# Polar factor of a 128x128 matrix: 32 Newton steps inside attention against 17 quintic steps in two later stages

## The reference, cut to what matters

```
x = x + attention(layernorm(x))        # 16 heads of 8, causal, 2 sequences
x = x + experts(layernorm(x))          # 16 experts, capacity N/16, top 1
x = x + scan_block(layernorm(x))
x = x + experts(layernorm(x))

# scan_block
U, _, Vt = svd(W_scan_raw);  W = U @ Vt          # 128 x 128: the polar factor
q = x @ W_up.T;  v = x @ W_v.T
q = scan over time with combine(left, right, W)  # v' = (left + right) @ W, attention over 4 lanes, rms norm
y = (q * v) @ W_proj.T
```

## Time and profile before

| | us |
|---|---|
| median of 3 runs | 1975.16 |
| lowest and highest of them | 1974.81, 1977.96 |
| the profiled execution: its own time | 1976.67 |
| the profiled execution: its span, first to last instruction | 1975.0 |
| mean granted clock of TensorE | 0.921 |

### The profile page before, as it was taken

The page is one execution under the profiler, slowest core; times in us unless marked ns, Lnnn a source line. Parts: engine busy times, 40 slices in busy tenths (PEclk is TensorE's granted clock), DMA queues, the critical chain, the costliest instruction groups (busy, mean ns, idle before and its releaser), DMA issues. The chain is left out here.

```text
span 1975.0 us, 42847 instructions
## 1 busy us (share of the span) xinstructions
PE 1624.5 (82%) x14150; PEld 1057.9 (54%) x14150; DVE 1423.3 (72%) x2559; ACT 952.3 (48%) x2093; POOL 688.7 (35%) x498
## 2 busy tenths in 40 slices
PE   4599989998998998999646648999999999976183
PEld 3233333333333333333435548888889888875173
DVE  6789988888988888987331246888888888874222
ACT  4177777777777776777421122333333333332020
POOL 5400000000000000000144326877777777853632
PEclk9699999999999999999857878999999999996597
DMA  3200000000000000000162151222222222204423
GB/s 115 83 18 19 18 15 16 18 19 20 19 19 12 18 19 20 19 18 2 70 217 73 44 147 35 86 76 79 79 85 78 80 76 85 85 22 147 153 68 104
DMA packets 171647, 117.12 MB, mean 59 GB/s; under 512 B 10940, under 2 KB 161852, under 8 KB 171208
## 3 DMA queue, kind: packets, MB, share of 16 engines
q1 hardware_dynamic: 167368, 106.33, 18.2%
q0 software_dynamic: 4096, 8.46, 1.2%
HBM read 63.98 MB, written 50.72 MB: 58 GB/s over the span
## 5 line engine op out<-in xcount | busy, mean ns | idle before, releaser
L562 DVE TENSOR_REDUCE chunk_max<-ps_max 128x1 f32<-128x512 f32 (+3 forms) x1280 | 703.8, 603 | 103.1 <-PE ps_max L667 56.6
L611 ACT ACTIVATE probs<-ps_s 128x512 f32<-128x512 f32 (+3 forms) x1280 | 612.6, 536 | 215.0 <-PE ps_s L659 106.5
L640 PE MATMUL ps_s<-Qs,Ks 50*128 50x512 bf16 (+3 forms) x1280 | 368.0, 353 | 37.9 <-DVE chunk_max L562 22.0
L650 PE MATMUL ps_max<-Ks,Qs 48*128 48x512 bf16 (+3 forms) x1280 | 377.3, 360 | 13.2 <-POOL a_ident L504 10.6
L712 PE MATMUL ps_o<-probs,Vp 128*32 128x512 f32 (+3 forms) x2560 | 343.9, 562 | 5.2 <-ACT O_sb L594 4.8
L1424 POOL TENSOR_TENSOR lane_products<-L,q 128x1024 f32<-128x1024 f32 x132 | 309.4, 2374 | 3.9 <-DMA L<-scanned 3.9
L519 POOL TENSOR_TENSOR A_b<-A_newton,b_tile 128x128 f32<-128x128 f32 x32 | 14.6, 457 | 811.3 <-ACT A_newton L614 811.3
L640 PEld LDWEIGHTS ps_s<-Qs,Ks 50*128 50x128 bf16 x1280 | 98.4, 93 | 370.0 <-DVE chunk_max L562 313.6
L1479 DVE TENSOR_TENSOR weighted<-exp_scores,psV_s 128x4096 f32<-128x4096 f32 x44 | 194.2, 4413 | 0.2 <-issue 0.2
L1437 POOL TENSOR_TENSOR q<-L,z_normed 128x1024 f32<-128x1024 f32 x44 | 141.5, 3216 | 144.5 <-DVE z_normed L1459 144.5
L1558 PE MATMUL psS<-ident,lane_products 128*128 128x128 f32 x1408 | 169.2, 279 | 23.9 <-POOL lane_products L1424 23.9
(11 more groups left out here) (224 smaller groups left out, 2317.8 us busy)
## 6 DMA issues: line engine op xcount, KB each, us to landing
scanned<-q SPq DMA_DIRECT2D x44, 512.0 KB
L<-scanned SPq DMA_DIRECT2D x44, 512.0 KB
m_w<-in_L_ffn_w_dram SPq DMA_DIRECT2D x32, 512.0 KB
Qs<-q_parts SPq DMA_DIRECT2D x192, 32.0 KB
Ks<-k_parts SPq DMA_DIRECT2D x192, 32.0 KB
dispatched<-m_blank SPq DMA_DIRECT2D x2, 2080.0 KB
m_blank<-dispatched SPq DMA_DIRECT2D x16, 260.0 KB
routed<-m_blank SPq DMA_DIRECT2D x2, 2048.0 KB
```

Source lines behind the costliest of these rows:

```text
L562: nc.vector.tensor_reduce(out, scores[:, 0:w], axis=AX.X, op=ALU.max).then_inc(max_reduced, 1)
L611: nc.scalar.activation(dst, ps_s[(k + r) % R][:, q0:], ACT.Exp, scale=SCALE).then_inc(exp_done, 1)
L640: last = nc.tensor.matmul(ps_s[(k + r) % R][:, q0:], K[r][rows, kt * P:(kt + 1) * P], Q[r][rows, g * QW + q0:(g + 1) * QW], start=True, st ...
L650: last = nc.tensor.matmul(ps_max[(k + r) % R][:, 0:w], Q[r][rows, i * P:(i + 1) * P], K[r][rows, ck * QW:ck * QW + w], start=True, stop=no ...
```

## The change

The Newton steps and everything that belongs to them leave `attend`. A class `Polar` computes 17 quintic steps of the same form with other coefficients, 14 with (3.4445, -4.7750, 2.0315) and then 3 with (15/8, -10/8, 3/8). In one step the copy of A, Z, Y and the copy of S are on VectorE, the copy of the transpose on ScalarE, the four matmuls on TensorE; GpSimd only makes two scaled identities. `moe` m0 runs 12 steps: on VectorE behind `route(1)`, on ScalarE behind `copy_totals(1)`, on TensorE behind `count(1)` and before the first `turn`. `scan_inputs` runs 5: on TensorE behind the turned weights; on VectorE two in front of the first moments and one in front of each of the other three groups of eight tiles; on ScalarE in front of the root. The second expert layer gets an empty list of steps.

```diff
-NEWTON = (15 / 8, -10 / 8, 3 / 8)
+SPREAD = (3.4445, -4.7750, 2.0315)
+SETTLE = (15 / 8, -10 / 8, 3 / 8)
+POLAR = [SPREAD] * 14 + [SETTLE] * 3
+POLAR_FIRST = 12
...
# attend, gpsimd
-            nc.gpsimd.memset(b_tile[:], NEWTON[1])
-            nc.gpsimd.tensor_scalar(a_ident[:], c.ident[:], NEWTON[0], None, ALU.mult).then_inc(made, 1)
...
-                    nc.gpsimd.tensor_tensor(A_b[:], A[:], b_tile[:], ALU.mult).then_inc(newton_pool, 1)
-                    pool.wait_ge(newton_pool, s * 2 + 1)
-                    nc.gpsimd.tensor_tensor(Z[:], A_b[:], a_ident[:], ALU.add).then_inc(newton_pool, 1)
# attend, vector
-                    if k == NEWTON_AA + 1 and exp:
-                        newton(s)
# attend, scalar
-                            nc.scalar.activation(A[:], newton_ps[:, 0:D], ACT.Copy).then_inc(misc_read, 1)
...
-                            nc.scalar.activation(c.S[:].rearrange("p a d -> p (a d)"), newton_ps, ACT.Copy)\
-                              .then_inc(misc_read, 1)
# attend, tensor
-                if k == NEWTON_A:
-                    misc("A")
-                    nc.tensor.matmul(newton_ps[:, 0:D], c.S[:, 0, :], c.S[:, 0, :], start=True, stop=True)\
-                      .then_inc(newton_mm, 1)
-                if k == NEWTON_AA:
-                    misc("Y")
-                    nc.tensor.matmul(newton_ps[:, 0:D], A[:], A[:], start=True, stop=True).then_inc(newton_mm, 1)
-                if k == NEWTON_X:
-                    nc.tensor.matmul(newton_ps[:, 0:D], c.S[:, 1, :], Y[:], start=True, stop=True)
-                    nc.tensor.matmul(newton_ps[:, D:], Y[:], c.S[:, 1, :], start=True, stop=True).then_inc(newton_mm, 1)
...
+class Polar:
+    def on_gpsimd(self, pool):
+        for step, t in self.scaled_ident.items():
+            self.nc.gpsimd.tensor_scalar(t[:], self.c.ident[:], step[0], None, ALU.mult).then_inc(self.made, 1)
+
+    def on_vector(self, dve, i):
+        vector, (_, b, a2) = self.nc.vector, self.steps[i]
+        dve.wait_ge(self.made, 2)
+        dve.wait_ge(self.A_in_psum, i + 1)
+        vector.tensor_copy(self.A[:], self.ps_A).then_inc(self.A_read, 1)
+        vector.scalar_tensor_tensor(out=self.Z[:], in0=self.ps_A, scalar=b, in1=self.scaled_ident[self.steps[i]][:],
+                                    op0=ALU.mult, op1=ALU.add).then_inc(self.A_read, 1)
+        dve.wait_ge(self.AA_in_psum, i + 1)
+        dve.wait_ge(self.A_read, 2 * i + 2)
+        vector.scalar_tensor_tensor(out=self.Y[:], in0=self.ps_AA, scalar=a2, in1=self.Z[:], op0=ALU.mult, op1=ALU.add)\
+              .then_inc(self.Y_done, 1)
+        dve.wait_ge(self.X_in_psum, 2 * i + 1)
+        vector.tensor_copy(self.c.S[:, 0, :], self.ps_X).then_inc(self.S_copied, 1)
+
+    def on_scalar(self, act, i):
+        act.wait_ge(self.X_in_psum, 2 * i + 2)
+        self.nc.scalar.activation(self.c.S[:, 1, :], self.ps_XT, ACT.Copy).then_inc(self.ST_copied, 1)
+
+    def on_tensor(self, pe, i):
+        tensor, S, S_T = self.nc.tensor, self.c.S[:, 0, :], self.c.S[:, 1, :]
+        if i:
+            pe.wait_ge(self.S_copied, i)
+        tensor.matmul(self.ps_A, S, S, start=True, stop=True).then_inc(self.A_in_psum, 1)
+        pe.wait_ge(self.A_read, 2 * i + 1)
+        tensor.matmul(self.ps_AA, self.A[:], self.A[:], start=True, stop=True).then_inc(self.AA_in_psum, 1)
+        pe.wait_ge(self.Y_done, i + 1)
+        if i:
+            pe.wait_ge(self.ST_copied, i)
+        tensor.matmul(self.ps_X, S_T, self.Y[:], start=True, stop=True).then_inc(self.X_in_psum, 1)
+        tensor.matmul(self.ps_XT, self.Y[:], S_T, start=True, stop=True).then_inc(self.X_in_psum, 1)
+
+    def tensor_done(self, pe):
+        pe.wait_ge(self.S_copied, len(self.steps))
+        pe.wait_ge(self.ST_copied, len(self.steps))
...
# moe: banks are the four halves of psH
+            if polar_steps:
+                polar.on_gpsimd(pool)               # before the blank rows are made
...
             route(1)
+            for i in range(len(polar_steps)):
+                polar.on_vector(dve, i)
...
             pe.wait_ge(steps_done, 5 + HALF_STEPS + 7)
+            if polar_steps:
+                pe.wait_ge(xsT_copied, NCH)
+                for i in range(len(polar_steps)):
+                    polar.on_tensor(pe, i)
+                polar.tensor_done(pe)
...
# scan_inputs, vector
+            for i in range(NPOLAR - SC + 1):
+                polar.on_vector(dve, i)
             for ch in range(SC):
+                if ch:
+                    polar.on_vector(dve, NPOLAR - SC + ch)
                 dve.wait_ge(summed, ch + 1)
...
# scan_inputs, tensor
             pe.wait_ge(wT_copied, 2)
+            for i in range(NPOLAR):
+                polar.on_tensor(pe, i)
+            polar.tensor_done(pe)
```

More of the change, by code:

```diff
@@ L440, in reads @@
             if not isinstance(s, int) or s > 0:
-                order = ["rows1", "A", "comb", "Y", "rows0", "X", "end"]
+                order = ["rows1", "comb", "rows0", "end"]
                 if not nxt:
                     order.remove("rows0")
-                return s * 6 + order.index(name)
-            return ["rows0 of head 0", "rows1", "A", "Y", "rows0", "X", "end"].index(name) if s == 0 else 0
+                return s * 3 + order.index(name)
+            return ["rows0 of head 0", "rows1", "rows0", "end"].index(name) if s == 0 else 0
         @block.sync
@@ L547, in normalise @@
                   .then_inc(misc_read, 1)
-            def newton(s):
-                dve.wait_ge(newton_mm, s * 3 + 2)
-                dve.wait_ge(newton_pool, s * 2 + 2)
-                nc.vector.scalar_tensor_tensor(out=Y[:], in0=newton_ps[:, 0:D], scalar=NEWTON[2], in1=Z[:],
-                                               op0=ALU.mult, op1=ALU.add).then_inc(misc_read, 1)
             def section(s, j, r, p, exp, nxt):
@@ L762, in between @@
                 if k == COMBINE_FIRST:
-                    misc("X")
+                    misc("end")
                     combine(s, 0)
-                if k == NEWTON_X:
-                    nc.tensor.matmul(newton_ps[:, 0:D], c.S[:, 1, :], Y[:], start=True, stop=True)
-                    nc.tensor.matmul(newton_ps[:, D:], Y[:], c.S[:, 1, :], start=True, stop=True).then_inc(newton_mm, 1)
             def section(s, j, r, p, exp, nxt):
@@ L830, in _, with __init__ @@
             dve.wait_ge(y_done, NCH)
+class Polar:
+    def __init__(self, nc, c, sb, sem, steps, banks):
+        self.nc, self.c, self.steps = nc, c, steps
+        self.A, self.Y, self.Z = (sb(n, [P, D]) for n in ("A_polar", "Y_polar", "Z_polar"))
+        self.scaled_ident = {step: sb(f"ident_{n}", [P, D]) for step, n in ((SPREAD, "spread"), (SETTLE, "settle"))}
+        self.ps_A, self.ps_AA, self.ps_X, self.ps_XT = (bank[:, 0:D] for bank in banks)
+        (self.made, self.A_in_psum, self.A_read, self.AA_in_psum, self.Y_done, self.X_in_psum, self.S_copied,
+         self.ST_copied) = (sem(n) for n in ("polar_made", "A_in_psum", "A_read", "AA_in_psum", "Y_done", "X_in_psum",
+                                             "S_copied", "ST_copied"))
+    def on_gpsimd(self, pool):
[32 more added lines that the diff above has]
+        pe.wait_ge(self.ST_copied, len(self.steps))
@@ L905, in moe @@
         y_sent = [sem(f"y_sent{u}") for u in range(2)]
+        polar = Polar(nc, c, sb, sem, polar_steps, [psH[0][:, 0:512], psH[0][:, 512:], psH[1][:, 0:512], psH[1][:, 512:]])
         block = cx.enter_context(nc.Block())
@@ L1071, in _ @@
             copy_totals(1)
+            for i in range(len(polar_steps)):
+                polar.on_scalar(act, i)
             def copy_rows(e):
@@ L1232, in scan_inputs @@
             sem(n) for n in ("xn_ready", "xT_in_psum", "xT_copied", "q_in_psum", "v_in_psum", "q_copied", "v_copied"))
+        polar = Polar(nc, c, lambda n, shape: sb(n + "_b", shape), sem, POLAR[POLAR_FIRST:],
+                      [psQ[:, 0:512], psQ[:, 512:], psV[:, 0:512], psV[:, 512:]])
+        NPOLAR = len(POLAR) - POLAR_FIRST
         block = cx.enter_context(nc.Block())
@@ L1255, in _ @@
         def _(pool):
+            polar.on_gpsimd(pool)
             for ch in range(SC):
```

28 lines of the change are left out of this document (6 added, 22 removed).

## The result

The changed kernel takes 1998.95 us (median of 4 runs, 1996.04 to 2000.16) and the kernel before 1976.47 (4 runs beside it, 1974.81 to 1977.96). The ratio is 1.011, interval 1.0098 to 1.0122: 22.5 us slower, where I had forecast 11.7. The profiled execution took 1999.71 us around a span of 1997.7.

A forecast was written before the change was run, and what follows sets the result against it. No engine was busy throughout; VectorE's row maxima set the attention's pace. Attention -11.4, first expert layer +8.0 and scan inputs +15.1 gave +11.7 us, taking the 1975.16 median to 1986.9; range 1981 to 1991, extended down to 1977.

The forecast's parts named there:

- part 1: Attention: removing 32 Newton steps saves 0.34 us a head for 31 heads, plus start and end: -11.4 us, bounds 0 to -25.5.
- A, Y and X: Three Newton places in each attention head, whose removal was to save 0.04, 0.10 and 0.20 us.
- The start: In front of the attention loop, TensorE no longer waits for the scaled identity: 0.4 us saved, bounds 0 and 0.6.
- the last head: Attention's final head, with no maxima to hide Newton work under: 0.5 us saved, bounds 0 and 1.3.
- nothing is added here, so a loss is excluded: Attention: claim that removing the Newton steps could not cost time, so the gain's lower bound was 0.
- The price of a step: One serial polar step: three matmul legs of 0.90 us and three VectorE operations of 0.28, 3.54 us; 2.61 at higher clock.
- part 2: First expert layer: 12 polar steps outlast the 34.0 us hole before the first gathered tile: +8.0 us, bounds 0 and 10.
- Part 3: Scan's input stage: 5 polar steps in VectorE's queue delay the moments: +15.1 us, bounds 11.4 and 16.
- The clock: TensorE's granted clock in both polar chains was taken to stay at 0.50, the 1.2 GHz level; forecast there given 0.79.
- the first rival: Clock rises in both polar chains, hiding the expert-layer steps and cutting the scan's cost to 11.4: 1975 us; chance 0.11.
- The second rival: Attention: Newton matmuls cause the whole of the 0.33 and 0.23 us gaps, saving 25.5 us: 1972.8 us; chance 0.06.
- the third: Scan's moments hide the polar steps, which then cost VectorE 4.2 us instead of 15.1: 1976 us; chance 0.04.

The follow-up runs named there:

- e1: Changed kernel with all 17 polar steps left out, only the Newton removal kept: 0.9989 of the kernel before, -2.2 us.
- e16: Changed kernel with 70 already-met waits on TensorE in the fourth and fifth heads of the attention loop's body: 1.0087 of the kernel before.
- e9: Changed kernel with 64 semaphore increments at the start of TensorE's attention stream: 1.0208 of the kernel before.
- e14: Changed kernel with 64 semaphore increments at the start of TensorE's attention stream, repeated on another chip: 1.0104 of the kernel before.
- e7: Changed kernel with its 17 steps spread over four places (2, 9, 3, 3); intended empty instructions absent from the built program: 0.9998 of the kernel before.
- e15: Changed kernel with its 17 steps spread over four places (2, 9, 3, 3), no padding, on another chip: 0.9988 of the kernel before.
- e10: Changed kernel with 128 semaphore increments at the start of TensorE's attention stream: 1.0296 of the kernel before.
- e11: Kernel before with 96 semaphore increments at the start of TensorE's attention stream: 1.0078 of the unpadded kernel before.
- e12: Changed kernel with steps spread over four places (2, 9, 3, 3) and 64 semaphore increments on TensorE in the attention: 1.0139 of the kernel before.
- e2: Changed kernel keeping the 12 steps of the first expert layer, the 5 beside the scan's moments left out: 1.0033 of the kernel before, +6.5 us.

## Why the prediction was wrong

**The size of part 1 is the step that failed.** I had -11.4 us; alone it measured -2.2 (e1). That lies within the bounds written beside the term, 0 and -25.5, but the range of the forecast kept only -8 to -16 of them. The working behind it was sound for a plain head: A, Y and X were to give 0.04, 0.10 and 0.20, and the traces of all the kernels with the new attention show 0.03 to 0.04, 0.08 and 0.19, at those steps, 0.30 for 0.34. The start (0.1 to 0.9 us earlier over the traces, for 0.4) and the last head (0.5 where no stall falls into it) came near the forecast too. What was wrong is "nothing is added here, so a loss is excluded": I multiplied one head by 31 and never looked at the heads that hold the turn of the loop, though the earlier trace rows give 26.70 as the average and the timeline of a plain head 26.15. The difference, some 17 us in all, was the loop's turn, and that loss grew with the changed stream of instructions by 4.2 us in the traced run and by 6.5 in e1. In the traced run 3.2 of the 4.2 are in the last heads of the passes, where the stall is, and the rest in the heads behind them. That a fetch delays a 4 KB store, and the store TensorE, is shown by e16 and the late pairs of all traces; that the turn is dearer when a fetch comes just ahead of it rests on three built streams with that pattern (e9 and e14, e16, e7 and e15), and is argued. Why TensorE stands idle a second time behind the turn in e10, e11 and e12 stays open, and so does the rest of what e1 lost: its attention ended 2.8 us ahead of the kernel before, and its last instruction 0.2 us behind.

**The price of a step** was 3.54 us and is 3.61: the leg of A takes 0.91 from matmul to VectorE, the other two 0.84, and each hop from VectorE to TensorE 0.34. Twelve of them make part 2 8.7 instead of 8.0, in the trace and in the runs (e2 less e1).

**Part 3** was 15.1 and is 14.9 in the trace, 16.2 in the runs. The order of the steps and the moments is as forecast: 7.1 us in front of the first bn_stats (1149.24 to 1156.38), then 4.1 us from group to group.

**The clock** stayed at 0.50 in both chains from the second matmul on, so the first rival is out. Around the first, the clock had risen for 3.4 us, from 1008.3 to 1011.7, where the kernel before had 0.50 throughout. The forecast tied this rival to what the Trainium skill says of copies, TensorE: Matmul & The Clock Gate (Loop structure matters more than you think): that they don't break the warmth. The changed kernel hardly tests it, since TensorE was idle for 2.8 us between the first A and the next matmul. The three steps behind the last expert do, and the traces differ. They began at 2.4 GHz with steps of 2.68 us (2.61 forecast). In e7 all three ran so, but in e15, the same built program, the second step's last matmuls were at 1.2 GHz again, from 1123.12 on, though no idle time of TensorE between was over 0.7 us. So a chain that once runs fast need not stay fast here.

**The second rival** (the gaps close wholly) is out with 0.30 us a head, and **the third** with the 14.9 us of part 3.

**A term I didn't have** is where the low clock falls in stages that the change doesn't touch. In the changed kernel it met the scan's tail:
```profile
1786.60:1790.00 3.40, 3.40 (x19) 3.40 (x18) 1.85 (x4) 1.06 (x3) 0.84 (x1) 0.50 0.00 0
```
The same stretch of the kernel before, for comparison:
```profile
1786.60:1790.00 3.40, 2.29 (x18) 2.05 (x17) 1.22 (x1) 1.02 (x1) 2.03 (x1) 0.90 0.00 0
```
The scan took 598.2 to 602.5 us over the traces, and the expert loop took from 0.9 us less to 2.2 more than in the kernel before. With the turns this may be why one profile can be 3 us off a median. It is an explanation that fits the rows; no run tested it.

The sum with the measured terms: -2.2 + 8.7 + 16.2 = 22.7, against 22.5. The sign and two of the three terms held. The range did not: the lower bound of part 1, no gain at all, stood in the text and would have given 1975.16 + 8.0 + 15.1 = 1998.3, but the range ended at 1991.

## What to carry to other kernels

Read a loop's gain in the passes, not in its plain part: count the heads that hold the turn separately, and treat their cost as unknown by several us for any change to TensorE's stream there, because its instruction fetches can hold up small transfers that someone waits for. A serial chain costs its full length beyond its cover and nothing within it: 17 steps at 3.6 us cost 24 us in two places and some 2.5 us in four by the traces, because the gaps were counted first. And before an experiment with padding is believed, count the instructions in the built program, and run it beside the kernel that it is to be compared with.

## What the runs showed of the hardware that I had not expected

- A 4 KB store of sixteen 256-byte packets was held up by 2.2 us when its last packet came through only behind a 16 KB instruction fetch of 0.93 us. Over 18 traces all 317 loads that went out over 1.5 us behind their store had such a fetch beside them.
- A semaphore increment issued by TensorE took about 0.16 us (64 of them from 70.39 to 80.26 in e9), a wait that is already met nothing that could be seen: 35 of them in a head left it at 25.86 us.
- One kernel took 1.0208 times the kernel before on one chip and 1.0104 on another, each time with a narrow interval. What differed was VectorE taking up TensorE's results 3 us late while GpSimd issued scatters, 18.9 of the some 20.6 us; a cause within the chip is not shown. A ratio measured on one chip is not safe from that if only one of the two kernels has such a chain.
